# A four-layer graph network on one core: the edge attributes' product in two edge loops, split into four products on 64 rows

## Time and profile before

| | |
|---|---|
| median of 3 runs | 13133.17 us (13126.07 to 13138.51) |
| the profiled execution, its span | 13179.5 us |
| PE matmul busy | 4527.1 us, 34% |
| PE weight load busy | 3022.1 us, 23% |
| VectorE busy | 6535.8 us, 50% |
| GpSimd busy | 8151.7 us, 62% |
| the three passes of `edge_pass` | 2275, 2272 and 2273 us |

### The profile page before, as it was taken

How to read it: one execution, slowest core, us unless ns; L and a number is a source line. 1 busy time by engine, 2 the same in 40 slices (tenths; PEclk the granted TensorE clock), 3 DMA queues, 4 the chain that set the end, 5 groups by cost and what they waited for, 6 DMA issues and landing times. The chain is left out here.

```text
span 13179.5 us, 81573 instructions
## 1 busy us (share of the span) xinstructions
PE 4527.1 (34%) x15877; PEld 3022.1 (23%) x15877; DVE 6535.8 (50%) x10237; ACT 1994.5 (15%) x4360; POOL 8151.7 (62%) x8551
## 2 busy tenths in 40 slices
PE   3354455555222222232222222222222234434443
PEld 3244344444110111111111111111111123333332
DVE  9543344444544454454445455444544544444445
ACT  3233333333100000010000000000000022222223
POOL 1455555555676666656666666766666666666665
PEclk7555555555555555555555555555555555555555
DMA  2355555555333333323333332333333222222222
GB/s 76 106 155 154 149 152 155 153 159 152 99 86 82 87 89 87 88 72 85 87 87 93 81 91 79 87 85 88 89 87 86 81 58 66 69 68 68 68 69 63
DMA packets 1007936, 1264.02 MB, mean 96 GB/s; under 512 B 483123, under 2 KB 740467, under 8 KB 1007331
## 3 DMA queue, kind: packets, MB, share of 16 engines
q0 software_dynamic: 303696, 520.91, 17.5%
q1 hardware_dynamic: 638139, 635.93, 14.8%
q10 hardware_dynamic: 65600, 101.96, 2.7%
HBM read 829.46 MB, written 428.44 MB: 95 GB/s over the span
## 5 line engine op out<-in xcount | busy, mean ns | idle before, releaser
L789 POOL DMA_INDIRECT e_got<-kv_tab,dst_cols x1661 | 1574.5, 948 | 1281.7 <-DVE e_pay L894 770.2
L1843 POOL DMA_INDIRECT e_got<-h_tab,src_tcols x1612 | 1540.9, 956 | 881.8 <-issue 473.8
L1151 POOL DMA_INDIRECT e2a_got<-x_tab,src_cols x1616 | 1531.3, 948 | 775.7 <-issue 556.2
L1151 POOL DMA_INDIRECT e_got<-x_tab,src_cols x1616 | 1553.5, 961 | 718.3 <-issue 586.9
L1151 POOL DMA_INDIRECT e2b_got<-x_tab,src_cols x1616 | 1531.3, 948 | 745.7 <-issue 518.8
L1168 PE MATMUL e2b_EA<-we_W_edge,e2b_attr 128*128 128x384 f32 x808 | 574.9, 866 | 1331.2 <-DVE e2b_emsg L1187 728.3
L1168 PE MATMUL e_EA<-we_We,e_attr 128*128 128x384 f32 x808 | 578.3, 871 | 1297.8 <-issue 898.1
L1168 PE MATMUL e2a_EA<-we_W_edge,e2a_attr 128*128 128x384 f32 x808 | 572.0, 862 | 1300.4 <-issue 767.3
L894 DVE TENSOR_TENSOR e_pay<-e_got,e_Q 128x384 f32<-128x384 f32 x416 | 230.2, 553 | 1570.4 <-ACT e_Q L962 1129.1
L1940 DVE TENSOR_TENSOR_SCAN e_run<-e_Z,e_run,e_msg 98x512 f32<-98x512 f32 x404 | 516.9, 1279 | 795.4 <-ACT e_msg L2005 619.8
L805 PE MATMUL e_Q<-e_window,e_pick 128*128 128x96 f32 x3328 | 758.9, 408 | 79.1 <-issue 41.2
(11 more groups left out here) (373 smaller groups left out, 10316.0 us busy)
## 6 DMA issues: line engine op xcount, KB each, us to landing
scan_out<-e_out SPq DMA_DIRECT2D x416, 200.0 KB
e_window<-q_tab SPq DMA_DIRECT2D x1664, 48.0 KB
scan_out<-e_out SPq DMA_DIRECT2D x404, 196.0 KB
scan_out<-e_out SPq DMA_DIRECT2D x202, 384.0 KB
scan_out<-e2a_out SPq DMA_DIRECT2D x202, 384.0 KB
scan_out<-e2b_out SPq DMA_DIRECT2D x202, 384.0 KB
e_rel<-rel_row ACTq DMA_DIRECT2D x208, 256.0 KB
e_keep<-keep_row ACTq DMA_DIRECT2D x208, 200.0 KB
```

The source lines that it names most:

```text
L789: e.indirect_dma_start(got[i][:, k, :], None, kv_tab, bass.IndirectOffsetOnAxis(dst_c[:, c * K + k:c * K + k + 1], axis=0)).then_inc(s_g[i ...
L1151: e.indirect_dma_start(got[s % RS][:, k, :], None, x_tab, bass.IndirectOffsetOnAxis(src_cols[:, q:q + 1], axis=0)).then_inc(edge_got[s % R ...
L1843: e.indirect_dma_start(got[c % RG][:, k, :], None, h_tab, bass.IndirectOffsetOnAxis(src_tcols[:, q:q + 1], axis=0)).then_inc(s_g[c % RG], 16)
```

## The change

The weights become 128 rows by 192 columns: two block diagonals of 64 x 192, one over the other. The attributes are laid out otherwise by the host, outside the launch, with the same number of bytes. Each step makes four products instead of two: for each of two sets of 128 attribute columns, one on rows 0 to 63 that writes bank 0 of `EA`, and one on rows 64 to 127 that writes bank 1. Each streams 192 columns. The edges end up in the same places of `EA` as before, and the add reads the same addresses; only the names in its pattern change. Waits and counters stay as they were: `t_attr` is raised once, by the fourth product.

```diff
-        we = {n: keepb("we_" + n, [P, K * D]) for n in ("We", "W1_edge", "W2_edge")}
+        we = {n: keepb("we_" + n, [P, 2 * D]) for n in ("We", "W1_edge", "W2_edge")}
...
                 for k in range(K):
-                    loads.append((we[n][k * DE:(k + 1) * DE, k * D:(k + 1) * D], t[key]))
+                    loads.append((we[n][k * DE:(k + 1) * DE, k % 2 * D:(k % 2 + 1) * D], t[key]))
...
                             for h in range(2):
-                                ins = e.matmul(EA[s % 2][:, h, 0:K * D], attr[s % RA][:, h * P:(h + 1) * P], edge_w[:, :], start=True, stop=True)
+                                for r in range(2):
+                                    at = slice(r * 2 * DE, (r + 1) * 2 * DE)
+                                    ins = e.matmul(EA[s % 2][:, r, h * 2 * D:(h + 1) * 2 * D], attr[s % RA][at, h * P:(h + 1) * P], edge_w[at, :],
+                                                   start=True, stop=True)
                             ins.then_inc(t_attr, 1)
...
-                            e.tensor_tensor(emsg[s % 3][:, :, :].rearrange("p (h k) d -> p h (k d)", h=2), EA[s % 2][:, :, 0:K * D],
-                                            got[s % RS][:, :, :].rearrange("p (h k) d -> p h (k d)", h=2), ALU.add).then_inc(v_add, 1)
+                            e.tensor_tensor(emsg[s % 3][:, :, :].rearrange("p (r k) d -> p r (k d)", r=2), EA[s % 2][:, :, 0:K * D],
+                                            got[s % RS][:, :, :].rearrange("p (r k) d -> p r (k d)", r=2), ALU.add).then_inc(v_add, 1)
...
-    attr_S = np.ascontiguousarray(attr_pad.reshape(4, NCH // 2, P // 4, 2, K, DE).transpose(1, 4, 5, 3, 0, 2).reshape(NCH // 2, K * DE, 2 * P))
+    attr_S = np.ascontiguousarray(attr_pad.reshape(4, NCH // 2, P // 4, 2, 2, 2, DE).transpose(1, 3, 5, 6, 4, 0, 2).reshape(NCH // 2, K * DE, 2 * P))
```

## The result

The changed kernel takes **13,216.6 us** (median of 5, 13,189.14 to 13,236.43), the kernel before 13,138.51 us beside it (median of 5): ratio **1.0052, 95% interval 1.0041 to 1.0064**. It is slower by 78 us. Slower is the side that the prediction took, but it said 15,700 us, 2,570 us more than before. The time lies within the range.

What follows compares the result with a forecast made beforehand. It took TensorE's late attribute signal, 1.40 us per weight load or matmul, to bound each 11.25 us step; 15.7 us a step added 2,600 to 13,180 us, 15,780 us profiled, 15,700 us median, range 12,350 to 18,000 us.

Steps and rivals of the forecast that it cites:

- The add is late for `t_attr`, and a record costs 1.40 us in the flow.: Add waits for the attribute products' signal, 1.40 us per weight load or matmul of any width; 23.5 us a step at most.
- The real work of TensorE is hidden, the memsets, the add and the load cost nothing.: TensorE's 1.5 to 4.3 us a step lies under the gathers; it, the start memsets, add and attribute load count 0.
- 10.0 us of gathers and some 3.5 us until they have drained and the signals run free: Each step: 13.5 us signals 9.6 records at 1.40 us, then 7.2 at 0.31 us take 2.2 us: 15.7 us.
- 3.5 + 2.2 = 5.7 us: Each step's waiting beyond the gathers: 3.5 us until signals run free, 2.2 us for the remaining 7.2 records.
- 10.0 us of gathers: GpSimd's eight gathers a step, taken as the pace when signals are prompt, 9.97 us measured early in a pass.
- 2,600 us: Total slowdown: 4.45 us more a step over 570 to 600 of the 606 steps.
- its lower end 1,060 us: Smallest slowdown, if signals run free at once behind the last gather: 13.0 us a step.
- free rate of 0.31 us a record: Signal price without gathers, read at the first pass's end: 16 records in under about 5 us.
- The rival "same": A limit of 11.25 us a step outside TensorE, so the number of records changes nothing: 13,133 us, chance 0.27.
- the two counts that give 1.400 exactly: Four-step distances of adds, 47.60 us / 34 and 50.40 us / 36 records, held as evidence against no change.
- The rival "faster": Signals follow TensorE's shortened work and fall under 10.0 us a step, gathers set the pace: -760 us, 12,370 us, chance 0.30.
- a pass does run at 9.97 us when signals are prompt, so the gain is there to be had: Evidence for a faster kernel: the first 12 steps' adds follow at the gathers' pace, 11 steps in 109.6 us.

Runs made afterwards that it cites:

- experiment 1: Kernel before with each attribute product cut in two by columns, 16 weight loads and matmuls a step, nothing side by side: ratio 1.0001 in a prompt job, 1.0052 late.
- experiment 3: Kernel before with one, two, four tiny extra products a step in the three passes: 11,240.31 us prompt; 13,181.22 against 13,144.84 us late.
- experiment 2: Kernel before with attribute products repeated 2, 3, 4 times by pass: 11,248.67 us prompt; 2, 3, 6 times: 13,331.75 against 13,143.68 us late.
- experiment 4: Kernel before with 4, 4, 2 attribute weight loads and matmuls a step in the three passes: 11,249.46 us prompt; 13,079.24 against 13,143.68 us late.
- experiment 6: Kernel before with both products of all passes made in bf16 from upper word halves, 4 records a step: 13,097.93 against 13,144.84 us late, ratio 0.9959.
- experiment 5: Kernel before with less traffic, two late runs: fewer gathers or no attribute loads, 11,063.58 us; half-row, seven or memset-spaced gathers, 12,890.89 us.
- k13: Kernel before, late: 64 rows a gather in the first pass, seven gathers a step in the second, a memset after each gather in the third: 12,890.89 us.
- k11: Late run of the kernel before with each attribute product cut in two by columns: 13,217.61 against 13,144.84 us, ratio 1.0052.
- k14: Kernel before with both products of all three passes made in bf16 from upper word halves, late: 13,097.93 against 13,144.84 us, ratio 0.9959.
- k15: Kernel before with six buffers for the gathered rows in place of three, prompt: ratio 1.0001.
- k17: Kernel before with a memset of 256, 384, 768 columns after each gather by pass, prompt: 11.54, 12.39 and 14.95 us a step.
- k1_columns: Prompt run of the kernel before with each attribute product cut in two by columns: 11,242.61 against 11,240.54 us, ratio 1.0001.

## Why the prediction was wrong in size

- *The add is late for `t_attr`, and a record costs 1.40 us in the flow.* Right for a single long step: 22.40 us for 16 records occur after the change, and with column halves and with half of the records tiny (experiments 1, 3). With 24 and 48 records the price no longer holds (experiment 2), and of a pass it says nothing.
- *The real work of TensorE is hidden, the memsets, the add and the load cost nothing.* Right as far as it shows: experiment 1 has 0.5% without the row halves, and prompt runs have 0.0% with them.
- *The step that failed: "10.0 us of gathers and some 3.5 us until they have drained and the signals run free", 15.7 us for every step.* It pays the waiting for the quiet once a step and adds it to the gathers. The trace after shows one quiet for a whole spell of steps: after steps of 20 to 22.4 us the gathers are held for 5.69 us, the signals due come at once, and steps of 5.5 us make up for it. Over the second pass after, the gathers' starts lie 258 us further apart in sum than at 1.25 us each, nearly all of it in 49 holds for 202 steps: 1.3 us a step, where the sum had 3.5 + 2.2 = 5.7 us. In before it was 237 us already, 1.2 us a step. The earlier trace rows had this in them (two loads 1.4 us apart, with the vector engine behind), and I read a rate off it where a mean over a spell of some eight steps was wanted.
- *Under it lies "10.0 us of gathers".* That is GpSimd's issue time, and the earlier trace rows show it while the pass is young (109.6 / 11 is 9.96 us, not 9.97). Over a pass a late job gives no less than 1.384 us for each gather, 11.07 us a step, when there are almost no records to wait for (experiments 4, 6), and 1.405 us when the signals are prompt (experiment 5, third pass of `k13`). So a held-back gather loses little: in the account that fits, the queued gathers are worked off in that time. The 11.24 us of before were within 0.17 us of this floor, and what 8 more records add is 0.09 us, 54 us in all, where the sum had 2,600 us and even its lower end 1,060 us.
- *The free rate of 0.31 us a record* was read from one add too few. The two adds that the 16 records release stand at 5705.16 us and at 5711.54 us, so the row allows up to 12.8 / 16 = 0.8 us a record. The error that mattered lies in the step above, not here.

```profile
5711.54 0.92 DVE L1187 TENSOR_TENSOR e_emsg<-e_EA,e_got 128x768 f32<-128x768 f32 x1
```

- *The rival "same"* named the right thing, "a limit of 11.25 us that is not TensorE's at all and shows itself through `t_attr`, for example one shared with the gathers". It was weighed down by "the two counts that give 1.400 exactly"; both are true at once. The equal passes in the earlier trace rows were the better evidence: a mean over 202 steps against two stretches of four.
- *The rival "faster"* had "a pass does run at 9.97 us when signals are prompt, so the gain is there to be had". In a late job it is not: with adds that waited for no signal a pass ran at 11.08 us. In prompt jobs both kernels already have it.

What is shown: the count of records is the cause of the 0.5% and its size is not their work or rows; in late jobs a floor of 1.384 us for each gather instruction, not for rows; no lateness without gathers; a step of 11.2 us with prompt signals too. What is argued only: that one server works on gathers and records in turn, and that a held-back gather is no loss because the server still has gathers queued. It fits the table and seven gathers, but the test with deeper buffers met no late job, and the spaced gathers of `k13` (11.24 us) do not fit it fully. What the server is stays open.

## What to carry to other kernels

Where two engines wait for each other through buffers, a price read off a few steps is not the price of a pass: take the mean over all steps, and if passes with different counts take the same time, look for the floor that they share before adding anything. To find the floor, take away the suspected cost in one pass and see which other wait comes in its place. And ask of a late signal whether it makes up for it later: only what the floor leaves idle is lost.

## What the runs showed of the hardware

- The same kernel took 13,140 or 11,240 us from job to job (17% apart, with each job's own runs within 0.7%). It is not fixed by the chip: of two jobs on the same chip one was late (`k11` to `k14`) and one prompt (`k15` to `k17`). In late jobs it is not only these passes: the stretch from 440 us to the first pass takes 3,000 us in the trace of before and 2,236 us in the prompt trace of `k1_columns`.
- In late jobs weight loads and matmuls are signalled 1.40 us apart while gathers flow at 1.25 us, a gather takes at least 1.384 us in the mean of a pass, and both are without regard to size. Every run here wrote a record of each instruction. The Trainium skill, "NOTIFIC — the notification-queue block", section "Overflow: three behaviours, one of which stalls the engine", says that the block which writes such records holds up its producers inside rather than lose one. A price for each record would fit that; no run here went without records, so it is not shown. The number of records alone does not make a job late: the late trace of before and the prompt one of `k15_deep_before` both hold 81,573 instructions. If it is the records, the 0.5% is a cost of being looked at.
